# Softmax sums as an extra column of the weighted sum, turned on VectorE, and both halves of a batch weighed together one step later

## The reference, cut to what matters

```python
q, k, v = jnp.split(h @ W_qkv.T + b_qkv, 3, axis=-1)      # to 32 x 16 heads x 128 tokens x 8
scores = jnp.einsum('bhqd,bhkd->bhqk', q, k) / math.sqrt(DH)
attn = jax.nn.softmax(scores, axis=-1)
o = jnp.einsum('bhqk,bhkd->bhqd', attn, v)
o = o.transpose(0, 2, 1, 3).reshape(B, P, H)
o = o @ W_o.T + b_o
```

## Time and profile before

| | us |
|---|---|
| median of 3 runs | 344.03 |
| lowest, highest | 340.81, 345.67 |
| the profiled execution | 341.98 |
| its span in the trace | 340.2 |
| PE busy | 301.8 (89%) |
| DVE busy | 265.8 (78%) |
| ACT (ScalarE) busy | 183.8 (54%) |
| POOL busy | 171.7 (50%) |

### The profile page before, as it was taken

One profiled execution on the slowest core, in us unless ns is written; L12 is line 12 of the kernel. 1 busy time (PEld: TensorE's weight loads), 2 busy tenths in 40 slices (PEclk: granted clock), 3 DMA queues, 4 the chain that ended last, 5 costly groups with the idle time before them and its releaser, 6 DMA issues.

```text
span 340.2 us, 10136 instructions
## 1 busy us (share of the span) xinstructions
PE 301.8 (89%) x3916; PEld 181.7 (53%) x3916; DVE 265.8 (78%) x625; ACT 183.8 (54%) x291; POOL 171.7 (50%) x332
## 2 busy tenths in 40 slices
PE   3989998998987689999898989878877999999994
PEld 2444444554544357676767676767555454444441
DVE  5579999898899757888889888988876676666542
ACT  4346776786877356657665656556535333322330
POOL 8142686996976586373738382821143232333300
PEclk9999999999999779999999999999999999999998
DMA  7930000510410014152525243430000001111112
GB/s 262 297 65 3 1 1 7 137 54 15 133 46 3 5 43 120 50 137 69 139 66 137 70 118 90 118 89 6 9 4 6 1 0 31 31 33 31 32 33 62
DMA packets 26223, 21.69 MB, mean 64 GB/s; under 512 B 4384, under 2 KB 25536, under 8 KB 25920
## 3 DMA queue, kind: packets, MB, share of 16 engines
q1 hardware_dynamic: 25600, 20.11, 22.1%
q10 hardware_dynamic: 576, 0.94, 0.9%
HBM read 4.26 MB, written 2.10 MB: 19 GB/s over the span
## 4 chain that ended last, share of the span: by engine, by line
PE 69%; DVE 17%; issue 7%; POOL 3%; ACT 2%; ACTq 1%; DVEq 0%; POOLq 0%
PE psum L269 62%; DVE rinv L892 4%; DVE hid L831 3%; DVE mx L885 2%; PE psum L431 2%; PE psum L620 1%; PE psum L457 1%; DVE feat L894 1%; PE psum L532 1%; PE psum L465 1%; DVE x_tok L841 1%; POOL xn_tile L1062 1%; DVE stats L824 1%; DVE projT L899 1%; PE psum L577 1%
## 5 line engine op out<-in xcount | busy, mean ns | idle before, releaser
L885 DVE TENSOR_REDUCE mx<-psum 128x8 f32<-128x1024 f32 x64 | 77.7, 1217 | 18.6 <-PE psum L269 18.5
L716 ACT ACTIVATE probs<-psum 128x1024 f32<-128x1024 f32 x64 | 65.5, 1023 | 26.3 <-PE psum L269 26.3
L269 PE MATMUL psum<-w_early,h0T 128*128 128x512 f32 x128 | 70.5, 637 | 0.0
L269 PE MATMUL psum<-probs,v_pad 128*32 128x128 f32 x1024 | 53.8, 280 | 12.2 <-DVE feat L894 10.4
L269 PE MATMUL psum<-probs,ones_pad 128*32 128x128 f32 x1024 | 52.6, 275 | 0.0
L749 ACT ACTIVATE g_act<-psum,w_late 128x512 f32<-128x512 f32 x32 | 22.0, 688 | 46.5 <-PE psum L269 46.5
L269 PEld LDWEIGHTS psum<-probs,v_pad 128*32 128x32 f32 x1024 | 26.4, 110 | 28.8 <-issue 20.6
L892 DVE RECIPROCAL rinv<-psum 128x128 f32<-128x128 f32 x32 | 30.6, 956 | 6.4 <-PE psum L269 5.6
L269 PEld LDWEIGHTS psum<-probs,ones_pad 128*32 128x32 f32 x1024 | 31.7, 111 | 0.1
L1025 POOL CAST m_part<-mx 128x16 bf16<-128x16 f32 x32 | 6.3, 198 | 49.7 <-DVE mx L885 49.7
L269 PE MATMUL psum<-h2T,w_late 128*128 128x512 f32 x64 | 31.3, 605 | 0.0
(11 more groups left out here) (126 smaller groups left out, 551.9 us busy)
## 6 DMA issues: line engine op xcount, KB each, us to landing
q_st<-q_part SPq DMA_DIRECT2D x48, 128.0 KB
k_st<-k_part SPq DMA_DIRECT2D x48, 128.0 KB, 2.4
x_tok<-x SPq DMA_DIRECT2D x8, 256.0 KB, 8.8
out<-out_t SPq DMA_DIRECT2D x8, 256.0 KB, 2.2
w_late<-late SPq DMA_DIRECT2D x1, 1159.5 KB, 9.5
w_early<-early ACTq DMA_DIRECT2D x3, 256.0 KB, 5.8
k_st<-k_st SPq DMA_DIRECT2D x4, 128.0 KB, 5.0
q_st<-q_st SPq DMA_DIRECT2D x4, 128.0 KB
```

Source lines behind the costliest of these rows:

```text
L269: return nc.tensor.matmul(o, w, m, start=start, stop=stop, skip_group_check=shares)
L716: nc.scalar.activation(probs[:, n % 3, :, :, :].rearrange("p f j q -> p (f j q)"), psum[:, pair[0]:pair[1] + 1, :].rearrange("p a b -> p ( ...
L885: v.tensor_reduce(mx[:, c % 2, :, r, :], psum[:, pair[0]:pair[1] + 1, :].rearrange("p f (j k) -> p f j k", j=4), X_AXIS, ALU.max, negate=T ...
```

## The change

`ones_pad` goes, and with it half of the matmuls of W. `v_pad` gets a column of ones for each pair of heads (`ONES_AT`), and its windows (`WINDOW`) put two heads and two columns of sums into 32 rows; the two halves of a batch now write different columns of the bank instead of adding into the same. Since sums stand in other rows than the values they belong to, VectorE turns the bank by 32x32 blocks into `o_turn` (128x256 from PSUM), takes the reciprocal of its 16 columns of sums, multiplies into `o_norm`, and turns that back into `feat` (128x128). On PE both halves of W(b-1) now follow E1(b), and stand ahead of the projection; no W is between the projection and the turn of the maxima. On VectorE the reduction of M0 comes ahead of `normalize`. `probs` has four buffers instead of three. At the start VectorE sets the ones after both halves of `v_pad` are cleared, one of them by POOL.

```diff
--- before.py
+++ after.py
@@ -33,7 +33,11 @@
 STACKS = 3
 LEAD = 3
 VW = 32
+
+
 VPITCH = 160
+WINDOW = [0, 32, 80, 112]
+ONES_AT = [16, 49]
 PAIRS = [(1, 2), (3, 4), (5, 6)]
 AV_BANK, MISC_BANK, X_BANK = 0, 7, 0
 BF16_ONES = float(np.array([0x3f803f80], dtype=np.uint32).view(np.float32)[0])
@@ -214,13 +218,14 @@
         q_st = [sb(f"q_st{n}", [P, SLOTS, GT], BF16) for n in range(STACKS)]
         k_st = [sb(f"k_st{n}", [P, SLOTS, GT], BF16) for n in range(STACKS)]
         v_pad = sb("v_pad", [P, 2, GRP, NH // 4, VPITCH])
-        ones_pad = sb("ones_pad", [P, VPITCH])
         mx = sb("mx", [P, 2, 2, 2, 4])
         m_rest = sb("m_rest", [P, NH])
         m_part = sb("m_part", [P, 2, 2, 4, SLOTS], BF16)
         m_T = sb("m_T", [HROWS, 2, P], BF16)
-        probs = sb("probs", [P, 3, 2, 4, P])
-        rinv = sb("rinv", [P, P])
+        probs = sb("probs", [P, 4, 2, 4, P])
+        o_turn = sb("o_turn", [P, NH // 2, 32])
+        rinv = sb("rinv", [P, NH // 2, 2])
+        o_norm = sb("o_norm", [P, NH // 2, 2, DH])
 
         projT = sb("projT", [D, GRP, P])
         xc = sb("xc", [P, GRP, D])
...
@@ -399,19 +404,15 @@
                 g, s = b // GRP, b % GRP
                 pe.wait_ge(b_exp, 2 * b + r + 1)
                 if r == 0:
-                    pe.wait_ge(b_norm, b) if b else pe.wait_ge(a_h0T, B)
+                    pe.wait_ge(b_turn, b) if b else pe.wait_ge(a_h0T, B)
                     if s == 0:
                         pe.wait_ge(shared_set, SHARED["v", g] + 1)
                 for f in range(2):
                     i = f + 2 * r
                     for j in range(4):
                         rows = slice(VW * j, VW * (j + 1))
-                        mm(bank(AV_BANK)[rows, 0:P], v_pad[:, g % 2, s, j, VW * i:VW * (i + 1)], probs[:, (2 * b + r) % 3, f, j, :],
-                           i == 0, i == 3, True)
-                    for j in range(4):
-                        rows = slice(VW * j, VW * (j + 1))
-                        last = mm(bank(AV_BANK)[rows, P:2 * P], ones_pad[:, VW * i:VW * (i + 1)], probs[:, (2 * b + r) % 3, f, j, :],
-                                  False, i == 3, True)
+                        last = mm(bank(AV_BANK)[rows, r * P:(r + 1) * P], v_pad[:, g % 2, s, j, WINDOW[i]:WINDOW[i] + VW],
+                                  probs[:, (2 * b + r) % 4, f, j, :], i == 0, f == 1, True)
                 last.then_inc(b_av, 1)
 
             def taken_out(fill):
@@ -478,18 +479,17 @@
                 on, pre = 0 <= b < B, 0 <= b + LEAD < B
                 if on:
                     exp_scores(b, 0)
-                if 0 <= b - 1 < B:
-                    weigh(b - 1, 1)
                 if pre:
                     max_scores(b + LEAD, 0)
                 if on:
                     exp_scores(b, 1)
+                if 0 <= b - 1 < B:
+                    weigh(b - 1, 0)
+                    weigh(b - 1, 1)
                 if late_proj(b):
                     project(*late_proj(b))
                 if b in FRONT:
                     front(*FRONT[b])
-                if on:
-                    weigh(b, 0)
                 if 0 <= b + LEAD - 1 < B:
                     transpose_max(b + LEAD - 1)
                 if pre:
@@ -668,7 +668,7 @@
                     if g >= 2:
                         act.wait_ge(b_av, 2 * GRP * (g - 1))
                     if g == 0:
-                        act.wait_ge(v_const_set, 3)
+                        act.wait_ge(v_const_set, 2)
                     nc.scalar.copy(v_pad[:, g % 2, :, :, :].rearrange("p s j (i c) -> p (s j) i c", c=VPITCH // 4)[:, :, :, 0:DH],
                                    bank(MISC_BANK).rearrange("p (sj i d) -> p sj i d", i=4, d=DH)).then_inc(shared_set, 1)
                 elif name == "q":
@@ -711,9 +711,9 @@
                 n = 2 * b + r
                 pair = PAIRS[OWNER[FILL_AT["exp", b, r]]]
                 act.wait_ge(b_s2, n + 1)
-                if n >= 3:
-                    act.wait_ge(b_av, n - 2)
-                nc.scalar.activation(probs[:, n % 3, :, :, :].rearrange("p f j q -> p (f j q)"),
+                if n >= 4:
+                    act.wait_ge(b_av, n - 3)
+                nc.scalar.activation(probs[:, n % 4, :, :, :].rearrange("p f j q -> p (f j q)"),
                                      psum[:, pair[0]:pair[1] + 1, :].rearrange("p a b -> p (a b)"), ACT.Exp,
                                      scale=DH ** -0.5).then_inc(b_exp, 1)
 
@@ -758,10 +758,10 @@
             v.memset(ones[:, :], 1.0).then_inc(const_set, 1)
             v.memset(zero_b[:, :], 0.0).then_inc(const_set, 1)
             v.memset(m_part[:, :, :, :, :].rearrange("p n f u h -> p (n f u h)"), 0.0).then_inc(const_set, 1)
-            v.memset(v_pad[:, 0, :, :, :].rearrange("p s j c -> p (s j c)"), 0.0).then_inc(v_const_set, 1)
-            v.memset(ones_pad[:, :], 0.0).then_inc(ones_zero_set, 1)
-            dve.wait_ge(ones_zero_set, 1)
-            v.memset(ones_pad[:, :].rearrange("p (i c) -> p i c", i=4)[:, :, 0:DH], 1.0).then_inc(v_const_set, 1)
+            v.memset(v_pad[:, 0, :, :, :].rearrange("p s j c -> p (s j c)"), 0.0).then_inc(v_zero_set, 1)
+            dve.wait_ge(v_zero_set, 2)
+            for at in ONES_AT:
+                v.memset(v_pad[:, :, :, :, :].rearrange("p n s j (h c) -> p (n s j) h c", h=2)[:, :, :, at:at + 1], 1.0).then_inc(v_const_set, 1)
 
             dve.wait_ge(first_loaded, 16)
             dve.wait_ge(t2_mm, 1)
@@ -888,10 +888,18 @@
             def normalize(b):
                 dve.wait_ge(b_av, 2 * b + 2)
                 if b:
+                    dve.wait_ge(b_prod, b)
+                v.transpose(o_turn[:, :, :].rearrange("p (t s) c -> p t s c", s=2),
+                            bank(AV_BANK)[:, 0:2 * P].rearrange("p (s t c) -> p t s c", s=2, c=32)).then_inc(b_turn, 1)
+                dve.wait_ge(b_turn, b + 1)
+                v.reciprocal(rinv[:, :, :], o_turn[:, :, 16:18]).then_inc(b_rinv, 1)
+                dve.wait_ge(b_rinv, b + 1)
+                if b:
                     dve.wait_ge(b_norm, b)
-                v.reciprocal(rinv[:, :], bank(AV_BANK)[:, P:2 * P]).then_inc(b_rinv, 1)
-                dve.wait_ge(b_rinv, b + 1)
-                v.tensor_tensor(tile_cols(feat, b), bank(AV_BANK)[:, 0:P], rinv[:, :], ALU.mult).then_inc(b_norm, 1)
+                v.tensor_tensor(o_norm[:, :, :, :], o_turn[:, :, 0:16].rearrange("p g (e d) -> p g e d", e=2),
+                                rinv[:, :, :].unsqueeze(3).to_broadcast([P, NH // 2, 2, DH]), ALU.mult).then_inc(b_prod, 1)
+                dve.wait_ge(b_prod, b + 1)
+                v.transpose(tile_cols(feat, b), o_norm[:, :, :, :].rearrange("p g e d -> p (g e d)")).then_inc(b_norm, 1)
 
             def gate_projection(g):
                 dve.wait_ge(c_proj_mm, g + 1)
@@ -928,10 +936,10 @@
                 last.then_inc(c_h2T, 1)
 
             def attention(b):
+                if 0 <= b + LEAD < B:
+                    maxima(b + LEAD, 0)
                 if 0 <= b - 1 < B:
                     normalize(b - 1)
-                if 0 <= b + LEAD < B:
-                    maxima(b + LEAD, 0)
                 g = (b + 8) // GRP
                 if b >= 0 and b % GRP == 0 and g < NG:
                     cast_q(g)
@@ -1032,7 +1040,7 @@
 
             p.memset(k_st[0][:, :, :].rearrange("p h t -> p (h t)").bitcast(F32), BF16_ONES).then_inc(stack_const_set, 1)
             p.memset(q_st[0][:, :, :].rearrange("p h t -> p (h t)").bitcast(F32), 0.0).then_inc(stack_const_set, 1)
-            p.memset(v_pad[:, 1, :, :, :].rearrange("p s j c -> p (s j c)"), 0.0).then_inc(v_const_set, 1)
+            p.memset(v_pad[:, 1, :, :, :].rearrange("p s j c -> p (s j c)"), 0.0).then_inc(v_zero_set, 1)
             pool.wait_ge(const_set, 6)
             rms(0)
```

More of the change, by code:

```diff
@@ L240, in build @@
             sem(n + "_loaded") for n in ("first", "up_gate", "up_val", "down", "late", "cond"))
-        const_set, eye_b_set, v_const_set, ones_zero_set, stack_const_set, perm_set = (
-            sem(n) for n in ("const_set", "eye_b_set", "v_const_set", "ones_zero_set", "stack_const_set", "perm_set"))
+        const_set, eye_b_set, v_const_set, v_zero_set, stack_const_set, perm_set = (
+            sem(n) for n in ("const_set", "eye_b_set", "v_const_set", "v_zero_set", "stack_const_set", "perm_set"))
         cond_mm, scale0_set, t1_set, t2_mm, t2_set, c_set, mods_mm, mods_set, bias_mm, bias_set = (
@@ L257, in build @@
         m_stacked = sems("m_stacked", 2)
-        b_s, b_max, b_m, b_s2, b_exp, b_av, b_rinv, b_norm = (
-            sem("b_" + n) for n in ("s", "max", "m", "s2", "exp", "av", "rinv", "norm"))
+        b_s, b_max, b_m, b_s2, b_exp, b_av, b_turn, b_rinv, b_prod, b_norm = (
+            sem("b_" + n) for n in ("s", "max", "m", "s2", "exp", "av", "turn", "rinv", "prod", "norm"))
         c_proj_mm, c_proj, c_res_mm, c_x2, c_stats, c_mv, c_var, c_rstd, c_xc, c_xn, c_xT, c_h2T, c_f2_mm, c_yT, c_y_mm, c_out = (
```

## The result

| | before | after |
|---|---|---|
| median, us | 344.03 | 376.04 |
| lowest, highest | 340.81, 345.67 | 373.90, 382.48 |
| span of the profiled execution | 340.2 | 376.4 |

The ratio is 1.094, 95% interval 1.087 to 1.101: the changed kernel is slower, by 32 us.

What follows compares the result with a forecast made beforehand. PE and VectorE were taken as nearly full in mid-attention, with waits between them. From the profiled 342.0 us, +12.3 - 0.5 + 1.0 - 0.5 + 0.5 + 2 gave 356.8, 357 us, range 347 to 369.

Steps and rivals of the forecast that it cites:

- E1: PE's fill by `exp_scores(b, 1)` in attention: waits for DVE's reduction of M1 of the step before, starts 0.05 us later.
- I put in one or two, +2: Attention: longer PE idling drops the clock in one or two steps, 1.4 us each, taken as +2 us.
- the terms outside them: Outside steps 4 to 22: steps 0 to 3 -0.5, steps 23 to 28 +1.0, last batches -0.5, start +0.5 us.
- the chain: Steps 4 to 22: exponentials, W, projection, save, turn, M1, reduction in a row; 5.2 us with q or k; +12.3.
- the clock drops in most groups: Rival, attention: eight to ten steps at 1.4 us more, +12 in place of +2, 367 us (361 to 372); chance 0.17.
- the projections run PE full three steps of four: Attention: the argument held against low clock in most groups, whose chance was put at 0.17.
- The turn's wait for the save: Each step with a projection: the turn of the maxima waits for ScalarE's save by some 0.7 to 0.9 us.
- VectorE's terms: Normalization on DVE: first turn 0.44, reciprocal 0.26, product 0.29, second turn 0.30; together 1.30 us against 1.20.
- no large term: Product beside POOL on DVE: steps with the cast of k vary by 0.3 us and no more; elsewhere slack hides it.
- the start and the way to the first turn: Kernel start: DVE waits for POOL's memset, at most 2.24 us, mostly under the loads of weights, taken +0.5.
- The save isn't last: Rival, attention steps: DVE's chain covers the save, 4.27 us a step, 343 us (338 to 350); chance 0.14.
- PE's time removed counts: Rival, attention steps: W off the path, 27 steps 0.4 to 0.6 us shorter, 331 us (327 to 337); chance 0.07.

Runs made afterwards that it cites:

- kept-warm kernel: Changed kernel plus matmuls nobody reads, 6 behind each projection and 7 or 14 ahead of `exp_scores(b, 1)`: 360.97 us, ratio 1.052.
- the PSUM runs: Turned block in PSUM instead of SBUF: changed kernel 380.95 us; layout and turns with the old order 339.20; W early and turn of the maxima early together 349.90.
- W early: Changed kernel with both halves of W(b-1) moved to directly behind `exp_scores(b, 0)`, ahead of M0: 349.37 us, ratio 1.019.
- the layout alone: Changed kernel's layout, turns and four `probs`, with PE's and VectorE's order of the kernel before: 340.16 us, ratio 0.986.
- half-back kernel: Changed kernel with W(b,0) back between the projection and the turn of the maxima, W(b-1,1) still ahead of the projection: 352.57 us, ratio 1.025.

## Why the prediction was wrong

**The step that failed is the clock.** "I put in one or two, +2" was the term. In steps 4 to 22 alone 14 of 19 had a clock under 1.00, and they cost 14.8 us (109.5 in the changed kernel, 94.7 with the clock kept at 1.00). The forecast had +14.8 us over before in all, and the spans differ by 36.2: of the 21.4 missing, 12.8 are this term in the 19 steps, 9.0 are the terms outside them, and the chain takes 0.4 back. The text itself had said that PE would idle 0.9 and 1.0 us a step and "more drops are likely"; it had the rival, "the clock drops in most groups", at 0.17. It held against it that "the projections run PE full three steps of four". Step 15 above shows that this is no protection: the projection itself ran at half clock, 2.06 us. The rival's price was also too low, 1.4 us a step against 1.64, because it took three pitches of W, 0.63, and 0.8 for the projection, where W lost 0.71 and the projection 0.93. Even the rival's 361 to 372 ends under the 376.

**The chain was right, to 0.4 us in 19 steps.** Forecast: 5.2 us for a step with q or k, measured 5.20 to 5.21 at full clock. Step with v and the one before it: 5.15 + 4.5 = 9.65, measured in the kept-warm kernel as 6.31 + 3.26 = 9.57; the share between the two differs, since the steps are cut at the turn of the maxima here and at the end of a reduction there. The 19 steps: 95.05 forecast, 94.7 at full clock. The turn's wait for the save: 0.77 to 0.87, forecast 0.87.

**VectorE's terms were right.** Groups by line, after:

```profile
L892 DVE STREAM_TRANSPOSE o_turn<-psum 128x256 f32<-128x256 f32 x32 | 14.4, 449 | 27.6 <-PE psum L274 27.6
...
L899 DVE TENSOR_TENSOR o_norm<-o_turn,rinv 128x128 f32<-128x128 f32 x32 | 14.3, 448 | 1.1
L902 DVE STREAM_TRANSPOSE feat<-o_norm 128x128 f32<-128x128 f32 x32 | 10.0, 311 | 1.1
L895 DVE RECIPROCAL rinv<-o_turn 128x16 f32<-128x16 f32 x32 | 8.1, 253 | 1.1
```

Forecast 0.44, 0.29, 0.30 and 0.26. Only the product is off, by contention, in the steps with the cast of k: at 202.07 it took 1.19 us beside POOL's 1.15. The Trainium skill, SBUF — State Buffer, Who interferes with whom, says that a DVE instruction with two SBUF inputs contends with a GpSimd instruction that reads SBUF; this and the PSUM runs bear it out. Giving it no large term was right too (380.95 without the contention).

**The other terms were all too low**, together 9.5 us against a forecast of 0.5: the start and the way to the first turn +2.9 (forecast +0.5), from there through step 3 +1.0 (-0.5), steps 23 to 28 +2.5 (+1.0), behind them +3.1 (-0.5). The clock has a part in most of them.

- The start: between 20 and 28 us of the span the granted clock was 0.65 and 0.50, and 1.00 before. VectorE's wait for the memset does make its first product `hid` start at 13.08 instead of 11.79. But in *W early*, with the same wait, it starts at 12.91, the clock there stays at 1.00, and the first turn stands at 111.95, as before the change. So the wait itself costs nothing by then. Why the clock fell there in this run is open.
- Steps 23 to 26 take 18.0 us, and 17.3 both before and in the kept-warm kernel: the forecast's chain, and in the changed kernel a clock of 0.80 and 0.77 in the first two. Step 27 takes 0.4 more than before, as forecast. Step 28 takes 6.37 instead of 5.00, at a clock of 0.73. The kept-warm kernel can't split that one, since its step 28 (7.73 us) has 14 added matmuls in it.
- Behind step 28 the kept-warm kernel is at +0.7, and no matmuls are added there; so most of the +3.1 is not the chain's. The first 18.5 us of it were at a clock of 0.75, and at 1.00 before.

**The other rivals.** "The save isn't last" fell: it was last in every step with a projection. "PE's time removed counts" fell here, but comes true in part where the order is kept: the layout alone is 1.4% faster, not the 4% of that rival, because the ring through the save takes 4.19 us in the steps with q or k, and VectorE is full in those with the cast of k (4.69 of 4.79 us). The rival's own condition, that neither the save nor E1's wait for M1 is late, is not met there: 0.29 and 0.20 us.

## What to carry over

Before an instruction is moved off a place where it seems to do nothing for the path, ask whose wait it fills: W was the cover of ScalarE's save, and half of it put back was worth 23 us. A new wait on PE can cost twice, once as a wait and once through the clock: where the loop repeats the wait, price the following work at the lower level for most of the loop too, as a case with a large chance. It need not come: the changed kernel lost 14.8 us in this way in 14 of 19 steps, *W early*, with waits about as long, had two such steps. Test a change of layout and a change of order apart; here one gained 1.4% and the other lost 17.8%.

## What the runs showed of the hardware

- Steps with the same work and the same waits on PE can be at different clocks. The changed kernel's step 11, 5.21 us with 3.46 busy and a bare save of 0.87, was at 1.00, and step 15, the same work, was at 0.75. The half-back kernel's steps of 4.76 us, 3.59 busy, all stayed at 1.00. *W early* had single waits of 1.81 us and a mean clock of 0.97 in mid-attention. In the changed kernel's steps 4 to 22 PE's longest wait was 2.0 us, and 14 of 19 were under 1.00. What decides is left open. The Trainium skill, TensorE: Matmul & The Clock Gate, A second HAM failure mode: psum-queue depth-cycling (HAM is its name for what sets the clock), tells of a kernel in which "the PE micro-idles between MM groups frequently enough that HAM oscillates". This trace agrees in that the clock goes to and fro between its two levels, 1.00 and 0.50 within step 15, with waits of 0.87 and 0.88 us; that such waits are enough it doesn't show, since step 11 has them at 1.00.
- A turn by 32x32 blocks on VectorE, in float32, took 449 ns in the mean for 128x256 from PSUM (438 in the layout alone) and 311 ns for 128x128 within SBUF. The Trainium skill, VectorE: DVE Perf Modes, The three transpose paths, has 311 ns for 128x128 in bfloat16, the same figure.
- A VectorE product of 128x128 with two sources in SBUF took 1.19 to 1.30 us when it started just behind a POOL operation of 1.15 or 1.16, and ended 0.15 us behind it; with one source in PSUM it took 0.29 beside the same operation.
